# Merge product of the feed-forward stage as three float32r products, with the output norm on VectorE

## The reference, cut to what matters

```python
merged = scaled.transpose(0, 2, 1, 3).reshape(B, S, 2 * E)   # 512 columns a row
a = merged @ Wo                                              # the merge product, 256 columns
x = x + _layernorm(a)
h = jnp.einsum('bsd,fd->bsf', _layernorm(x), _ternary(W1)) + b1   # 1024 columns
h = jax.nn.gelu(h, approximate=False)
out = jnp.einsum('bsf,df->bsd', h, _ternary(W2)) + b2
x = x + _layernorm(out)
```

## Time and profile before

| | us |
|---|---|
| median of 3 runs | 3715.27 (3708.71 to 3716.58) |
| the profiled execution | 3713.94 |
| its span, first to last instruction | 3712.2 |
| TensorE busy in the span | 3301.5 (89%) |
| VectorE, ScalarE, GpSimd busy | 2753.2 (74%), 2341.0 (63%), 1689.3 (46%) |
| `merge_and_ffn`, first transpose to last sum | 2284.05 to 2721.2 |

### The profile page before, as it was taken

The page is one execution under the profiler, slowest core; times in us unless marked ns, Lnnn a source line. Parts: engine busy times, 40 slices in busy tenths (PEclk is TensorE's granted clock), DMA queues, the critical chain, the costliest instruction groups (busy, mean ns, idle before and its releaser), DMA issues. The chain is left out here.

```text
span 3712.2 us, 68222 instructions
## 1 busy us (share of the span) xinstructions
PE 3301.5 (89%) x22302; PEld 2009.5 (54%) x22302; DVE 2753.2 (74%) x6822; ACT 2341.0 (63%) x4989; POOL 1689.3 (46%) x2994
## 2 busy tenths in 40 slices
PE   5888799999999999999999995999969978969940
PEld 4676344444444444444444443888847755648840
DVE  6776799999999999999999971666634537853358
ACT  4555377777777777777777773676735446635532
POOL 2420266666666666666666664111100004646742
PEclk9999799999999999999999997999979988989975
DMA  5777643444434343443444312222151114335668
GB/s 193 230 237 226 101 74 73 73 80 77 70 76 79 79 71 75 79 79 70 74 80 78 72 33 79 78 86 81 40 178 35 58 46 141 120 125 171 177 194 253
DMA packets 380345, 393.48 MB, mean 106 GB/s; under 512 B 121369, under 2 KB 294425, under 8 KB 377817
## 3 DMA queue, kind: packets, MB, share of 16 engines
q1 hardware_dynamic: 365688, 350.56, 38.7%
q0 software_dynamic: 13728, 37.77, 2.7%
q10 hardware_dynamic: 576, 0.79, 0.1%
HBM read 230.21 MB, written 157.15 MB: 104 GB/s over the span
## 5 line engine op out<-in xcount | busy, mean ns | idle before, releaser
L732 ACT ACTIVATE att_p<-att_st 128x512 f32<-128x512 f32 (+3 forms) x3072 | 1325.8, 492 | 472.7 <-PE att_st L669 453.1
L799 DVE TENSOR_REDUCE att_mcol<-att_ring 128x1 f32<-128x512 f32 (+3 forms) x3072 | 1483.0, 546 | 138.3 <-PE att_ring L647 109.7
L669 PE MATMUL att_st<-att_ops 99*128 99x512 bf16 (+3 forms) x3072 | 915.3, 328 | 4.3 <-ACT att_p L732 3.5
L644 PE MATMUL att_ring<-att_ops 96*128 96x512 bf16 (+3 forms) x3072 | 878.7, 331 | 27.0 <-DMA att_va<-values 23.5
L681 PE MATMUL att_pv<-att_p,att_va 128*32 128x512 f32 (+3 forms) x6144 | 602.3, 494 | 2.2 <-POOL att_p L788 1.8
L788 POOL TENSOR_SCALAR_AFFINE_SELECT att_p<-att_p 128x512 f32<-128x512 f32 x512 | 321.8, 634 | 592.6 <-ACT att_p L732 587.7
L669 PEld LDWEIGHTS att_st<-att_ops 99*128 99x128 bf16 x3072 | 284.9, 98 | 445.7 <-ACT att_p L732 278.6
L647 PE MATMUL att_ring<-c_mask,c_identb 128*128 128x128 bf16 x2048 | 434.2, 221 | 0.0
L644 PEld LDWEIGHTS att_ring<-att_ops 96*128 96x128 bf16 x3072 | 296.8, 98 | 206.4 <-DVE att_mcol L799 80.4
L681 PEld LDWEIGHTS att_pv<-att_p,att_va 128*32 128x32 f32 x6144 | 144.2, 108 | 273.0 <-ACT att_p L732 140.4
L647 PEld LDWEIGHTS att_ring<-c_mask,c_identb 128*128 128x128 bf16 x2048 | 202.5, 99 | 106.9 <-issue 1.3
(11 more groups left out here) (285 smaller groups left out, 5943.2 us busy)
## 6 DMA issues: line engine op xcount, KB each, us to landing
att_ops<-parts SPq DMA_DIRECT2D x1524, 64.0 KB, 3.3
parts<-prj_pt SPq DMA_DIRECT2D x128, 384.0 KB, 3.9
moe_work<-moe_rows SPq DMA_DIRECT2D x79, 260.0 KB, 3.0
values<-prj_vs SPq DMA_DIRECT2D x16, 1024.0 KB, 6.7
att_va<-values SPq DMA_DIRECT2D x64, 256.0 KB, 3.8
heads<-att_ofin SPq DMA_DIRECT2D x128, 128.0 KB, 2.4
ffn_os<-heads SPq DMA_DIRECT2D x16, 1024.0 KB, 5.0
moe_work<-x SPq DMA_DIRECT2D x32, 512.0 KB, 5.1
```

The lines of the kernel that those rows point to most:

```text
L644: ins = nc.tensor.matmul(ring[k % NB][:, 0:w], ops[0:KR, s, a, mp, i * P:(i + 1) * P], ops[0:KR, s, a, 2 + mp, c * GN:c * GN + w], start=T ...
L669: nc.tensor.matmul(stp[(t * NST + n) % NS][:, off:GN], ops[:, s, a, 2 + mp, j * P:(j + 1) * P], ops[:, s, a, mp, half * GN + off:(half + 1 ...
L732: act.activation(pr[:, g % R, b, off:GN], stp[(t * NST + n) % NS][:, off:GN], ACT.Exp, scale=SCALE).then_inc(exp_done, 1)
L799: v.tensor_reduce(mcol[:, t % 2, c, col:col + 1], ring[k % NB][:, 0:min(GN, (i + 1) * P - c * GN)], AX.X, ALU.max).then_inc(ring_read, 1)
```

## The change

- The merge product is three float32r products in place of one float32 product. ScalarE copies each transposed chunk from PSUM twice: to `mt` as float32r and to `mf` as float32. VectorE makes `ml = mf - mt` (`merged_low`). `merge(g, t)` sums `mt*woh + ml*woh + mt*wol`: 12 products in place of 4, and it waits for the four `ml` chunks (`ml_ready`) in place of the copies (`tp_copied`). `woh` and `wol` are made from `wo` once, at the start of the stage, and TensorE's first instruction waits for them.
- The output norm (`norm_out`) moves from ScalarE to VectorE, as four `tensor_scalar` of 128x256, directly after `low_part(g, 1)`; the small `scales(2, ..)` for it is gone.
- VectorE's order is new: `merged_low` of group g + 2 stands behind `finish_stats(g - 1)`, two chunks on either side of `low_part(g, 0)`. Ahead of the loop, all eight `merged_low` of groups 0 and 1 stand in front of `merged_stats(0)`.

```diff
@@ TensorE
-            pe.wait_ge(C["s_ffn"], 48)
+            pe.wait_ge(wo_rest, 1)
...
             def merge(g, t):
-                pe.wait_ge(tp_copied, turned(g, HC - 1))
+                pe.wait_ge(ml_ready, (g + 1) * HC)
                 if g and t % 2 == 0:
                     pe.wait_ge(ya_read, 4 * (g - 1) + 2 * (t // 2) + 2)
-                for c in range(HC):
-                    ins = nc.tensor.matmul(ya[t // 2][:, t % 2 * E:(t % 2 + 1) * E], mt[:, c, t * P:(t + 1) * P],
-                                           C["wo"][:, c], start=(c == 0), stop=(c == HC - 1))
+                for one, (a, w) in enumerate(((mt, woh), (ml, woh), (mt, wol))):
+                    for c in range(HC):
+                        ins = nc.tensor.matmul(ya[t // 2][:, t % 2 * E:(t % 2 + 1) * E], a[:, c, t * P:(t + 1) * P].bitcast(F32R),
+                                               w[:, c].bitcast(F32R), start=(one == 0 and c == 0), stop=(one == 2 and c == HC - 1))
@@ ScalarE
             def merged(g, c):
                 act.wait_ge(tp_ready, turned(g, c))
-                act.activation(mt[:, c], tp[c % 2][:], ACT.Copy).then_inc(tp_copied, 1)
+                if g and c == 0:
+                    act.wait_ge(ya_ready, g * GT)
+                act.activation(mt[:, c].bitcast(F32R), tp[c % 2][:], ACT.Copy)
+                act.activation(mf[:, c], tp[c % 2][:], ACT.Copy).then_inc(tp_copied, 1)
...
-            def norm_out(g):
...
+            act.wait_ge(C["s_ffn"], 48)
+            act.activation(woh[:].bitcast(F32R), C["wo"][:], ACT.Copy).then_inc(wo_round, 1)
...
-                    if n == 4 and g:
-                        norm_out(g - 1)
@@ VectorE
+            def merged_low(g, c):
+                v.wait_ge(tp_copied, turned(g, c))
+                v.tensor_tensor(ml[:, c].bitcast(F32R), mf[:, c], mt[:, c], ALU.subtract).then_inc(ml_ready, 1)
...
+            def norm_out(g):
+                power.receive(v, nth["c", g])
+                if g:
+                    v.wait_ge(out_ready, g)
+                for t in range(GT):
+                    v.tensor_scalar(yf[:, t], yb[:, t], mv[:, 2, t, 0:1], rstd[:, 2, t:t + 1], ALU.subtract, ALU.mult).then_inc(yf_ready, 1)
...
+            v.wait_ge(wo_round, 1)
+            v.tensor_tensor(wol[:].bitcast(F32R), C["wo"][:], woh[:], ALU.subtract).then_inc(wo_rest, 1)
+            for c in range(HC):
+                merged_low(0, c)
+            for c in range(HC):
+                merged_low(1, c)
             merged_stats(0)
...
                 if g:
                     finish_stats(g - 1)
+                if ahead:
+                    merged_low(g + 2, 0)
+                    merged_low(g + 2, 1)
+                low_part(g, 0)
+                if ahead:
+                    merged_low(g + 2, 2)
+                    merged_low(g + 2, 3)
+                low_part(g, 1)
                 if g:
-                    scales(2, nth["c", g - 1], y_scale)
-                for n in range(5):
+                    norm_out(g - 1)
+                for n in range(2, 5):
                     low_part(g, n)
```

More of the change, by code:

```diff
@@ L910, in merge_and_ffn @@
         xs = m.sb("xs", [P, 2, GT, E])
-        mt = m.sb("mt", [P, HC, GN])
+        mf, mt, ml = m.sb("mf", [P, HC, GN]), m.sb("mt", [P, HC, GN]), m.sb("ml", [P, HC, GN])
+        woh, wol = m.sb("woh", [P, HC, E]), m.sb("wol", [P, HC, E])
         x1, xn = m.sb("x1", [P, 3, GT, E]), m.sb("xn", [P, 2, GT, E])
@@ L919, in merge_and_ffn @@
         h_loaded, x_loaded, x_stored = m.sems("h_loaded", 2), m.sems("x_loaded", 2), m.sems("x_stored", 2)
[L920 to L923, removed]
+        (wo_round, wo_rest, ml_ready, own_steps, tp_ready, tp_copied, ya_ready, ya_scale, ya_read, x1_ready, x1_scale, xn_ready,
+         xl_ready, hid_ready, gelu_done, lo_ready, yo_ready, yo_read, yf_ready, out_ready) = (m.sem(n) for n in (
+            "wo_round", "wo_rest", "ml_ready", "own_steps", "tp_ready", "tp_copied", "ya_ready", "ya_scale", "ya_read", "x1_ready", "x1_scale",
+            "xn_ready", "xl_ready", "hid_ready", "gelu_done", "lo_ready", "yo_ready", "yo_read", "yf_ready", "out_ready"))
         power = Power(C, 0)
@@ L1121, in _ @@
                     norm_merged(g + 2)
-            norm_out(G - 1)
         @block.vector
@@ L1159, in finish_stats @@
                 if g:
-                    v.wait_ge(yf_ready, g)
+                    v.wait_ge(yf_ready, GT * g)
                 for n in range(2):
@@ L1166, in finish_stats @@
                 spread(2, lambda t: yb[:, t])
+            def norm_out(g):
[4 more added lines that the diff above has]
+                    v.tensor_scalar(yf[:, t], yb[:, t], mv[:, 2, t, 0:1], rstd[:, 2, t:t + 1], ALU.subtract, ALU.mult).then_inc(yf_ready, 1)
             def finish(g):
-                v.wait_ge(yf_ready, g + 1)
+                v.wait_ge(yf_ready, GT * (g + 1))
                 if g >= 2:
@@ L1208, in _ @@
             finish_stats(G - 1)
-            scales(2, nth["c", G - 1], y_scale)
+            norm_out(G - 1)
             finish(G - 1)
```

## The result

The changed kernel takes 3797.23 us (median of 4 runs, 3793.83 to 3800.16) and the kernel before, timed beside it, 3712.08 (4 runs, 3708.71 to 3716.58). The ratio is 1.0221, with an interval of 1.0202 to 1.0241: 2.2% slower. The profiled execution of the changed kernel takes 3795.34 us. Its span is 3793.6 and that of before 3712.2, so there are 81.4 us to account for. The forecast was +66.5, or 3780 us, in a range from 3759 to 3797; the median lies at the upper end of that range.

What follows compares the result with a forecast made beforehand. TensorE was taken as the bound, with VectorE's chain ending shortly after TensorE needs it. Wait 45, clock 19.5, start 7 and output norm -5 sum to 66.5 us on 3713.94, so 3780 us, range 3759 to 3797.

Steps and rivals of the forecast that it cites:

- The wait and its length: Merge 0 waits for `ml` behind VectorE's `yb` statistics; turn 28.8 us for 25.37, 45 us over 13 turns.
- The clock: After some 4 us of TensorE idle each turn the clock falls to 0.50; 1.5 us a turn, 19.5 us in all.
- both idles: TensorE idles of 2.29 us ahead of a merge and 2.28 in group 14, each followed by clock 0.50.
- two slow stretches a turn: Rival: the clock loss in each turn is 2.7 us, 35 in place of 19.5, giving 3797 us; chance 0.15.
- The merge's own saving: Twelve float32r products in place of four float32 ones save near 1.0 us of TensorE's turn.
- the rows: Profile timings used for product costs: float32 merge of one tile 1.54 us, down's float32r products 0.119 each.
- The start: Ahead of the loop, extra copies and `ml` delay group 0's statistics and first turns; between 5.5 and 7.5, taken as 7 us.
- The tail: Output norm leaving ScalarE shortens turns 14, 15 and the very end, with a faster last merge; -5 us.
- TensorE as the bound: Rival: VectorE reaches the four `ml` before merge 0, turn 24.4 us, kernel faster at about 3700; chance 0.04.
- The stall without the clock: Rival: merge 0 waits but the clock stays up or the slow stretch falls in the idle; 3760 us, chance 0.13.
- half the stall: Rival: the chain has 3 us of hidden slack, turn stays about 25.4 us, kernel about 3714; chance 0.03.

Runs made afterwards that it cites:

- e4: The changed kernel with 26 unused float32r products on TensorE ahead of merge 0's wait for `ml`; 1.0118 to the kernel before, turn 28.70 us.
- e3: The changed kernel with the four `ml` ahead of the sum and statistics of `yb` in VectorE's order; 1.0039 to the kernel before, turn 26.46 us.
- e10: The kernel before, unchanged, profiled once more on the chip of the last experiments; turn 25.37 us, convolution stage 335.3 us.
- e12: The kernel before, unchanged, profiled a further time; turn 25.38 us, convolution stage 335.3 us.
- e1: The kernel before with only the output norm moved to VectorE, merge left in float32; 0.9996 to the kernel before, turn 25.37 us.
- e6: The changed kernel without `ml` (second products take `mt`) and with one copy per chunk; 0.9968 to the kernel before, turn 24.61 us.
- e8: The changed kernel with one copy per chunk, `ml` straight from PSUM and earlier in VectorE's order, merges placed otherwise; 0.9987 to the kernel before, turn 24.44 us.
- e7: The changed kernel with group 1's four `ml` behind group 0's statistics and scales; 1.0213 to the kernel before, start 51.9 us.

## Why the prediction was right, and where its size was off

**The wait and its length: right.** The prediction gave 15.26 us from down to the end of the `yb` statistics; measured 2506.72 - 2491.46 = 15.26. It gave 3.15 for the four `ml` with the low part between; measured 2509.77 - 2506.72 = 3.05. It gave 10.4 from merge 0 to down; measured 2521.71 - 2509.77 = 11.94, less 1.6 lost in that turn by the clock, 10.3. It gave a turn of 28.8 at full clock; e4 has 28.70. e3 shows that the order, not the added work, is what costs. ScalarE's copies end before the third `ml`, as said, and no wait for `wol` appears.

**The clock: right in kind, too small.** This is the term that was mis-sized: "In a busy stretch of 3.4 us this loses 3.4 x (1 - 0.119 / 0.21) = 1.5 us", 19.5 over 13 turns, and e4 measured 2.03, 26.4 in all. The 1.5 came from the stretches after two idles of 2.3 us in one execution. The repeats of the same kernel show that one of these stretches was chance. This is the merge after the same idle of 2.29 us in e10, with a window from shortly after its start:

```profile
2300.55 7.15 PE L1001 MATMUL ffn_ya<-f_wo,ffn_mt 128*128 128x256 f32 x32 [2.29 <-ACT ffn_yn L1067]
```

```profile
2301.30:2304.70 3.40, 3.40 (x17) 3.02 (x16) 3.18 (x10) 0.02 (x1) 0.00 (x0) 1.00 0.22 29
```

The clock is 1.00 there, as it is in e12 and e1 at the same place, and the 32 records take 7.15 us, not 8.83. So after this idle the clock fell in one of four executions. After the 1.5 us of e3 it fell in none of 13 turns, and after the 3.7 us of the changed kernel in all 13. The other stretch, in the turn of group 14, comes 4 us earlier in that turn in both repeats, ahead of hidden 7, and the idle there is 0.71 us instead of 2.28. That 4 us are longer than both idles was a sound argument, but the two falls it rested on were weaker evidence than the prediction took them for.

After 3.7 us the slow stretch differs from turn to turn. In the turn shown it goes from 2511.1 to 2514.5. In the next it is twice as long, and some 1.6 us of it lie in the idle:

```profile
2538.40:2545.20 6.80, 5.18 (x20) 4.80 (x21) 4.66 (x10) 3.37 (x7) 0.02 (x1) 0.50 0.01 2
```

From merge 0 to the transposes behind merge 1 it would be 1.42 + 4 x 0.23 + 1.42 = 3.8 at full clock. It took 2515.20 - 2509.77 = 5.43 in the turn shown, where the first record of merge 0 is 0.74 long, and 2546.22 - 2540.01 = 6.21 in the next, where that record is 1.22 long because the clock is down from the first product on. Losses of 1.6 and 2.4, with the long kind in two turns of three (31.0, 30.9, 30.2), make a mean of 2.1, near e4's 2.03. The rival "two slow stretches a turn" (2.7) was thus nearer than the forecast's 1.5 in two turns of three, but it had no part of the stretch in the idle.

**The merge's own saving: about right.** Forecast near 1.0 a turn, measured 0.76 (e6), and 0.93 in e8, whose merges are placed otherwise. The Trainium skill, "FP8 and Floating Point Precision", section TensorE Precision Notes, has float32 as four passes, which gave 1.5 a turn in the prediction. e6 doesn't bear that out here: by the rows a float32 product takes 1.54 / 4 = 0.385 us and a float32r one 0.119, or 3.2 to 1, and the rows were the better guide.

**The start: about right.** 7 forecast, 7.9 measured, and 9.2 against the repeats. The statistics of group 0 start at 2301.16 for a forecast 2300.8, but the stage itself starts 1.8 us earlier here. Counted from the first transpose they are 18.92 - 11.29 = 7.6 us late, where the forecast had 5.4, and 1.5 more with the clock down. e7 shows 3.5 of the start to be the place of group 1's `ml`.

**The tail: right in sign, smaller.** -5 forecast, -3.4 measured (-2.9 against the repeats), and e1 alone gives much the same (59.9 to 56.3). The norm's four steps take 0.34 each for the 0.3 taken.

**The convolution: not foreseen.** +7.8 us in a stage whose instructions don't change; the prediction took the rest of the span as fixed. It and the clock in the turns (+6.9) are nearly the 15 us by which the span ended above the forecast; 0.9 and 1.6 come from start and tail, and the turns and the rest gave 1.8 and 0.5 back. The rival "two slow stretches a turn" gave 3797, and 3797.23 was measured, but that match is luck: it had 35 us of clock loss in the turns, where 26.4 were measured, and nothing in the convolution.

**The rivals.** TensorE as the bound fell at the place named: the `ml` ended 18.3 us after down. e8 shows that it holds once `ml` comes early. But e8 also has only one copy of each chunk, and the prediction didn't see that this is needed: with the order mended alone (e3), a turn is 26.46, and VectorE waits for ScalarE's second copy. The stall without the clock fell with e4, and half the stall with the turn of 30.73.

**Left open.** What decides when the clock comes back at the convolution's start. In the profiles it goes with the kernel, but no run here separates what TensorE did before from the chance of an execution.

## What to carry to other kernels

Before adding an operation to an engine that runs its queue in order, write down when the engine gets there, not how busy it is: VectorE had a third of each turn free, and four 0.6 us operations cost 3.3 us a turn because they stood behind a chain that ended too late, in a loop that passes the delay on. Once such a wait is there, ask which engine would hold the loop next (here ScalarE's second copy), because undoing the first alone gives only part back. And where an idle of TensorE bounds the loop, price it twice, once as time and once as the slower clock that may follow it. Before taking that second price from one execution, look at a repeat: here the same idle of 2.29 us was followed by the slow clock in one of four.

## What the runs showed of the hardware

A recurring idle of 3.7 us on TensorE was followed by a granted clock of 0.50 (1.2 GHz) in every turn, at 2.0 us a turn; 26 products in the idle, some 3.1 us of work that no one uses, kept it at 1.00 and made the kernel 1.0% faster. The Trainium skill, "TensorE: Matmul & The Clock Gate", section HAM oscillation, tells of a kernel in which the recurring wait for data brings the clock down at every step of its loop; the trace agrees, with a wait for another engine in place of one for data. Shorter idles are less certain: those of 1.5 us left the clock at 1.00 in all 13 turns of e3, and the one of 2.29 us ahead of the loop was followed by 0.50 in one of four executions (before, and not e1, e10 and e12).

The clock can also stay down while TensorE is fed. The first row is the changed kernel inside its convolution stage, from 33.4 us after its start; the second is the kernel before, from 33.8:

```profile
2832.00:2852.00 20.00, 19.20 (x46) 11.80 (x45) 6.16 (x22) 5.84 (x13) 1.64 (x1) 0.58 1.04 318
```

```profile
2760.00:2780.00 20.00, 16.66 (x68) 10.61 (x68) 7.75 (x25) 9.41 (x20) 1.64 (x1) 0.96 1.03 314
```

TensorE is busy for 19.20 of 20 us in the first with 46 products, and for 16.66 in the second with 68, at clocks of 0.58 and 0.96. A higher busy share is here the mark of the slower clock.
